# Scores on four 64x64 tiles of TensorE, stack transfers in halves, seven stretches of scores per batch

## The reference

```python
q = (x @ wq.T).reshape(Bx, Tx, H, Dh).transpose(0, 2, 1, 3)   # k, v likewise; H = 16, Dh = 8, Tx = 256
attn = jnp.einsum('bhqd,bhkd->bhqk', q, k) / scale
attn = attn + slopes[None, :, None, None] * dist[None, None, :, :]   # dist = -|key - query|
attn = jax.nn.softmax(attn, axis=-1)
out = jnp.einsum('bhqk,bhkd->bhqd', attn, v)
x = _layernorm(x + out.transpose(0, 2, 1, 3).reshape(Bx, Tx, H * Dh) @ wo.T + bo)
x = _layernorm(x + ffn(x))    # silu gate, two gelu layers, down projection
```

## Time and profile before

| | us |
|---|---|
| median of three runs | 845.25 (842.99 to 847.95) |
| the profiled execution | 847.85 |
| its span in the profile | 846.0 |

### The profile page before, as it was taken

The page is one execution under the profiler, slowest core; times in us unless marked ns, Lnnn a source line. Parts: engine busy times, 40 slices in busy tenths (PEclk is TensorE's granted clock), DMA queues, the critical chain, the costliest instruction groups (busy, mean ns, idle before and its releaser), DMA issues.

```text
span 846.0 us, 22833 instructions
## 1 busy us (share of the span) xinstructions
PE 795.7 (94%) x8322; PEld 582.6 (69%) x8322; DVE 632.1 (75%) x1298; ACT 607.0 (72%) x1099; POOL 311.4 (37%) x488
## 2 busy tenths in 40 slices
PE   4889998999999999998999979999999999999994
PEld 2556666667666666666666558888888888888873
DVE  4768897889888888887888355777777777777774
ACT  3557776767777777776777777777777777777762
POOL 3436776868655555656453310000000000000001
PEclk9999999999999999999999999999999999999997
DMA  6676677776666756676651100111111111111001
GB/s 176 132 159 137 167 155 168 151 172 147 153 139 148 156 146 151 135 159 134 160 128 30 52 21 30 33 37 37 37 37 37 37 33 35 33 36 38 26 26 51
DMA packets 102173, 81.21 MB, mean 96 GB/s; under 512 B 11840, under 2 KB 94912, under 8 KB 102080
## 3 DMA queue, kind: packets, MB, share of 16 engines
q1 hardware_dynamic: 100480, 76.59, 38.8%
q0 software_dynamic: 880, 2.88, 1.8%
q10 hardware_dynamic: 720, 0.46, 0.2%
HBM read 45.82 MB, written 33.55 MB: 94 GB/s over the span
## 4 chain that ended last, share of the span: by engine, by line
PE 91%; DVE 4%; issue 2%; DMA 1%; ACT 1%; SPq 0%; POOL 0%; DVEq 0%; POOLq 0%
PE ps_b L947 16%; PE ps_b L950 16%; PE ps_o L524 15%; PE ps_a L464 11%; PE ps_b L472 5%; PE ps_a L479 4%; PE ps_b L580 4%; PE ps_b L479 3%; DVE neg_sb L759 3%; PE ps_a L950 3%; PE ps_a L947 3%; PE ps_b L541 2%; PE ps_a L563 2%; PE ps_a L549 2%; PE ps_b L535 1%
## 5 line engine op out<-in xcount | busy, mean ns | idle before, releaser
L759 DVE TENSOR_REDUCE neg_sb<-ps_a 128x2 f32<-128x512 f32 x512 | 326.4, 684 | 72.4 <-PE ps_a L479 69.7
L653 ACT ACTIVATE probs<-ps_b 128x512 f32<-128x512 f32 x512 | 270.8, 594 | 90.3 <-PE ps_b L479 89.8
L464 PE MATMUL ps_a<-qk_stack 52*128 52x256 bf16 x1024 | 187.8, 277 | 21.4 <-DMA qk_stack<-qk_scratch 7.5
L472 PE MATMUL ps_b<-qk_stack 54*128 54x256 bf16 x1024 | 182.5, 273 | 0.8 <-ACT probs L653 0.8
L1042 ACT ACTIVATE gelu_f<-ps_b,sc 128x512 f32<-128x512 f32 x128 | 88.2, 689 | 76.8 <-PE ps_b L950 69.3
L479 PE MATMUL ps_a<-corner_sb,eye_sb 64*128 64x128 bf16 x1024 | 141.4, 220 | 0.0
L524 PE MATMUL ps_o<-probs,v_aug 128*32 128x256 f32 x2048 | 138.5, 387 | 1.1 <-issue 1.1
L479 PE MATMUL ps_b<-corner_sb,eye_sb 64*128 64x128 bf16 x1024 | 138.4, 216 | 0.0
L464 PEld LDWEIGHTS ps_a<-qk_stack 52*128 52x128 bf16 x1024 | 68.3, 95 | 90.2 <-issue 51.2
L1152 POOL TENSOR_SCALAR vareps_f<-meanvar_f 128x4 f32<-128x4 f32 x16 | 9.9, 617 | 319.4 <-DVE meanvar_f L1138 319.4
L479 PEld LDWEIGHTS ps_a<-corner_sb,eye_sb 64*128 64x128 bf16 x1024 | 97.7, 97 | 8.6
(11 more groups left out here) (112 smaller groups left out, 1459.8 us busy)
## 6 DMA issues: line engine op xcount, KB each, us to landing
qk_stack<-qk_scratch SPq DMA_DIRECT2D x62, 384.0 KB, 6.3
qk_scratch<-qk_sb SPq DMA_DIRECT2D x64, 192.0 KB, 2.3
qk_scratch<-qk_sb SPq DMA_DIRECT2D x96, 128.0 KB, 2.4
xT_sb<-in_xT SPq DMA_DIRECT2D x32, 128.0 KB, 4.0
qk_stack<-mrow SPq DMA_DIRECT2D x256, 2.0 KB
x_sb<-in_x SPq DMA_DIRECT2D x32, 128.0 KB, 3.7
x_scratch<-x_sb SPq DMA_DIRECT2D x32, 128.0 KB, 3.5
x_in<-x_scratch SPq DMA_DIRECT2D x32, 128.0 KB, 2.1
```

The costliest lines, as they stand in the source:

```text
L464: pe.matmul(ps[:, qb * SEQ:(qb + 1) * SEQ], q_stack[i][rows_of, j, qb * P:(qb + 1) * P], k_stack[i][rows_of, j, :], start=(qb == 0), stop= ...
L472: pe.matmul(ps[:, kb * SEQ:(kb + 1) * SEQ], k_stack[i][rows_of, j, kb * P:(kb + 1) * P], q_stack[i][rows_of, j, :], start=(kb == 0), stop= ...
L653: nc.scalar.activation(probs[:, h % HALF, :], ps_b[b_bank(t, k)][:], ACT.Exp, scale=slope[h]).then_inc(exp_done, 1)
L759: nc.vector.tensor_reduce(negmax[:, h_a // HALF, h_a % GROUPS, h_a % HALF // GROUPS, :], ps_a[a_bank(t, k)][:].rearrange("p (b k) -> p b k ...
```

## The change

Eight edits, all in the attention part:

1. Every score product is cut into two of 64 output partitions (`side` 0 and 1), for `score_max` and `score_exp` both, so a slot has eight matmuls of 256 columns in place of four. `add_corner` keeps its four matmuls of 128 columns, but each has 64 output partitions and a 64-wide unit matrix. All twelve go to 64x64 tiles.
2. `AT` is another table: `v` and `wo` behind slot 1 (and `wo` first), `turn norm` behind 8, `pv 1` behind 10, `qk` and `max 1` behind 13. The scores fall into seven stretches of 2, 3, 2, 2, 2, 3 and 2 slots.
3. `stack` moves a half of the heads in two transfers of 192 KB. The first half is issued where the stack was; the second half at the start of the next step, behind the maxima.
4. `spill(t + 3)` waits for the stacks of batch `t + 1` (the last that used this scratch buffer), no longer for those of `t + 2`.
5. `max_rows` issues two transfers of 4 KB in place of four of 2 KB.
6. ScalarE copies the first maxima behind its slot 3 (was 6), and the second behind slot 14 (was 12); q and k behind 13 (was 12).
7. VectorE adds the residual at slot 1 (was 2) and sums the statistics at 11 (was 5).
8. The last `wo` takes a bank by a rule of its own, since the table moved.

```diff
-AT = {"v": 2, "wo": 2, "pv 3": 4, "max 0": 6, "turn o": 6, "pv 0": 6, "turn norm": 9, "pv 1": 9, "qk": 12, "max 1": 12, "pv 2": 15}
+AT = {"v": 1, "wo": 1, "pv 3": 4, "max 0": 6, "turn o": 6, "pv 0": 6, "turn norm": 8, "pv 1": 10, "qk": 13, "max 1": 13, "pv 2": 15}
...
-            def stack(i, par):
...
+            def stack(b, half):
+
+                src = qk_dram[b % 2].rearrange("n r d (g h j) t -> h g (r d) n (j t)", g=GROUPS, h=2)
                 for g in range(GROUPS):
...
+                    dst = qk_stack[b % STACKS][g * TILE:g * TILE + STACK, :, half * HH:(half + 1) * HH, :]
+                    sp.dma_start(dst.rearrange("p n j t -> p n (j t)"), src[half, g]).then_inc(stacked[b % 2][half], DMA)
...
                 for r in range(MPARTS):
-                    for g in range(GROUPS):
-                        row = g * TILE + MROW + r
-                        dst = qk_stack[i][row:row + 1, 0, hf * HH:(hf + 1) * HH, :]
...
+                    dst = qk_stack[i][MROW + r:P:TILE, 0, hf * HH:(hf + 1) * HH, :]
+                    sp.dma_start(dst.rearrange("g h (b q) -> g (h b) q", b=BLK),
+                                 mrow[hf][:, r, :]).then_inc(m_landed[hf], DMA)
...
+                if live(t + 2, BATCH) and t + 2 > 0:
+                    stack(t + 2, 1)
...
                 if live(t + 3, BATCH):
-                    wait(sp, stacked, (t + 3) * GROUPS * DMA)
+                    for half in range(2):
+                        wait(sp, stacked[1 - par][half], (t + 3) // 2 * GROUPS * DMA)
                     spill(t + 3, 1 - par)
...
-            def score_max(ps, i, h, qb):
+            def score_max(ps, i, h, qb, side):
...
-                rows_of = slice(g * TILE, g * TILE + KA)
-                pe.matmul(ps[:, qb * SEQ:(qb + 1) * SEQ], q_stack[i][rows_of, j, qb * P:(qb + 1) * P],
+                rows_of, at = slice(g * TILE, g * TILE + KA), qb * P + side * TILE
+                pe.matmul(ps[side * TILE:(side + 1) * TILE, qb * SEQ:(qb + 1) * SEQ], q_stack[i][rows_of, j, at:at + TILE],
                           k_stack[i][rows_of, j, :], start=(qb == 0), stop=False, skip_group_check=True)
...
                 for half in range(BLK):
-                    if in_a:
-                        score_max(to_a, i_a, h_a, half)
-                    if in_b:
-                        score_exp(to_b, s, k, half)
+                    for side in range(2):
+                        if in_a:
+                            score_max(to_a, i_a, h_a, half, side)
+                        if in_b:
+                            score_exp(to_b, s, k, half, side)
...
-                    if k == 6 and live(t + 1, BATCH):
+                    if k == 3 and live(t + 1, BATCH):
                         copy_max(t, 0)
...
-                    if k == 12 and live(t + 1, BATCH):
+                    if k == 14 and live(t + 1, BATCH):
                         copy_max(t, 1)
...
-                    if k == 5 and live(t - 2, BATCH):
+                    if k == 11 and live(t - 2, BATCH):
                         sum_stats(t, par)
```

More of the change, by code:

```diff
@@ L121, in a_bank, with spare_bank @@
 def a_bank(t, use):
+    if (t, use) == (BATCH + 1, "wo"):
+        return next(i for i in range(A_BANKS) if i not in (a_bank(BATCH, "turn o"), spare_bank()))
     return (t * len(A_USES) + A_USES.index(use)) % A_BANKS
+def spare_bank():
+    return next(i for i in range(A_BANKS) if i not in (a_bank(BATCH, "wo"), a_bank(BATCH, "turn o")))
 def b_bank(t, use):
@@ L290, in attention @@
         spilled = sem("spilled")
-        stacked, half_stacked = sem("stacked"), sem("half_stacked")
+        stacked = [[sem(f"stacked{i}_{half}") for half in range(2)] for i in range(2)]
         v_done, v_copied = sem("v_done"), sem("v_copied")
@@ L307, in attention @@
         FIRST, LAST = -4, BATCH + 1
-        X_BANK = next(i for i in range(A_BANKS) if all(
-            a_bank(t, use) != i for t, use in ((BATCH, "wo"), (BATCH, "turn o"), (BATCH + 1, "wo"))))
+        X_BANK = spare_bank()
         pieces = []
@@ L405, in step @@
                         sp.wait_ge(rows_laid[t + 3], 2)
+                    stack(t + 3, 0)
                     if t + 3 == 0:
-                        stack_first(0)
-                        stack_first(1)
-                    else:
-                        stack((s + 3) % STACKS, 1 - par)
+                        stack(0, 1)
                 if t == BATCH - 1:
@@ L430, in take_a @@
             def take_a(t, use):
+                if (t, use) == (BATCH + 1, "wo"):
+                    wait(pe, res_done, BATCH - 1)
+                    return ps_a[a_bank(t, use)]
                 before = last_use(t, use, A_USES, A_BANKS, a_batch, FIRST)
@@ L487, in scores @@
                 if in_a:
-                    if h_a == 0 and b_a == 0:
-                        pe.wait_ge(half_stacked, GROUPS * DMA)
-                    elif h_a == (0 if b_a > 0 else HALF):
-                        wait(pe, stacked, (b_a + 1) * GROUPS * DMA)
+                    if h_a % HALF == 0:
+                        wait(pe, stacked[b_a % 2][h_a // HALF], (b_a // 2 + 1) * GROUPS * DMA)
                     to_a = take_a(t, k)
@@ L598, in step @@
                     scores(t, s, k)
+                    if k == AT["wo"] and live(t - 2, BATCH):
+                        project_out(t)
                     if k == AT["v"] and live(t, BATCH):
                         project_v(t)
[L601 to L602 removed]
                     if k == (3 if t < 0 else AT["max 0"]) and live(t + 1, BATCH):
@@ L670, in step @@
                         copy_oT(t)
-                    if k == 12 and live(t + 4, BATCH):
+                    if k == 13 and live(t + 4, BATCH):
                         wait(act, qk_done, t + 5)
@@ L761, in step @@
                                                 AX_X, ALU.max, negate=True).then_inc(max_done, 1)
-                    if k == 2 and live(t - 2, BATCH):
+                    if k == 1 and live(t - 2, BATCH):
                         if t == FLAG_AT:
@@ L820, in split_max @@
                 wait(pool, m_copied, b * 2 + hf + 1)
-                wait(pool, m_landed[hf], b * MPARTS * GROUPS * DMA)
+                wait(pool, m_landed[hf], b * MPARTS * DMA)
                 nc.gpsimd.tensor_copy(mrow[hf][:, 0, :], max_f[hf][:]).then_inc(m_first, 1)
@@ L1199, in shape_constants @@
     corner[:, :, 1, 0], corner[:, :, 1, 1] = above.T, above
-    eye = np.eye(P, dtype=np.float32).reshape(2, TILE, P).transpose(1, 0, 2)
     qscale = np.tile(1.0 / (np.array(slopes()).reshape(HG, GROUPS).T.reshape(-1) * np.sqrt(float(DH))), DH).astype(np.float32)
@@ L1204, in shape_constants @@
         "ident": np.eye(P, dtype=np.float32),
-        "eye": np.concatenate([eye] * GROUPS, 0),
+        "eye": np.tile(np.eye(TILE, dtype=np.float32), (GROUPS, 1)),
         "corner": corner.reshape(P, 2, 2, TILE),
```

32 lines of the change are left out of this document (10 added, 22 removed).

## The result

| | before | after |
|---|---|---|
| median, us | 844.12 (837.12 to 847.95) | 811.3 (810.1 to 813.78) |
| the profiled execution | 847.85 | 810.1 |
| its span | 846.0 | 808.3 |

The account below looks back on a forecast made before the run. TensorE's 13.36 us attention step, plus waits for maxima on SP's equally long loop, was taken as the bound; 847.85 - 23.0 (step) - 12 (waits) = 812.9, less 2.6 for the profiled execution: 810 us, range 797 to 838.

Parts of the forecast that it names:

- The slot: TensorE's scores: corners take one pass instead of two, so a slot falls from 0.335 to 0.285 us, 0.80 us a step.
- Rival (2): Weight loads of 64 columns cost like float32: slot 0.317 us, 829 to 836 us in all; chance 0.12.
- rival (4): Slower: row and column tiles together don't run side by side, loads or matmuls; 940 to about 1000 us; chance 0.10.
- The seventh stretch: TensorE leaves the scores once more in each attention step, charged at 0.08 us a step, between 0.03 and 0.15.
- VectorE's slack: VectorE's attention work, 11.9 us a step, fits the new step of 12.64 us with 0.7 us to spare.
- Rival (3): Slot falls but step doesn't, as VectorE or GpSimd and SP take over: steps 13.1 to 13.3 us, 824 us; chance 0.12.
- The waits: TensorE's waits for maxima at slots 0 and 8: 12 of 17.4 us gained, from below 5 to above 17.
- stand behind half as many bytes: Second-half maxima on the DMA engines: stack landing of 6.5 us ahead of them becomes some 3.3.
- The wait for the last stacks: SP's first-half maxima no longer stand behind this wait, up to 3.1 us.
- The fewer issues: SP issues each set of maxima in two in place of four, 1.35 us less; SP's step 10.2 us, below 12.64.
- the two terms: Attention gains added up: net 23.0 us from slot and seventh stretch over 32 steps, and 12 us of waits.
- The DMA engines' share of 0.66 rises to 0.72: DMA engines' busy share in the attention, with all bytes as before.

Follow-up runs that it names:

- six_stretches: Changed kernel with `turn norm` and `pv 1` behind slot 9, `qk` and `max 1` behind 12, `pv 2` behind 14, ScalarE's copies to match: 814.3 us.
- halves_together: Changed kernel with both halves of a stack issued together where the whole stack was, four transfers of 192 KB: 810.9 us.
- whole_stacks: Changed kernel with a stack read back whole again, two transfers of 384 KB with 4 KB packets in the old place: 837.0 us.
- spill_waits_last: Changed kernel with the old, stricter wait: the spill of batch t + 3 waits also for both halves of the stack of t + 2: 825.2 us.
- maxima_alone: Kernel before with the maxima in two transfers and nothing else: 833.2 us.
- transfers_alone: Kernel before with only edits 3 to 5 (stacks in halves, relaxed spill wait, maxima in two issues): 828.5 us.
- tiles_alone: Kernel before with only edit 1, the twelve 64x64 matmuls a slot; old table, transfers and slots: 853.6 us.

## Why the forecast was right, and where its reasons were not

**The slot** was forecast at 0.285, a gain of 0.80 us a step: it is 0.278 (from 0.334), 16 x 0.056 = 0.90. The load was taken as near 94 ns and is 106; hidden, as argued. Rival (2), a slot of 0.317, and rival (4), tiles or loads one behind the other, are out by the row at 278.71.

**The seventh stretch** was forecast at 0.08 us: 7 x 0.123 - 6 x 0.102 = 0.25. The way out of a stretch had been taken as unchanged, and it grew. Before, a bank wait of some 0.07 us stood in slots 13 to 15, which I had not seen. 0.90 - 0.25 + 0.07 = 0.72, which is the 0.73 found: 22.6 us against 23.0 forecast. Two errors of 0.1 cancelled.

**VectorE's slack**: 338 of 370 us busy, and the step still 12.63. Rival (3) is out. Where it binds is not in the sum but at single banks, as `six_stretches` shows.

**The waits** were forecast at 12 of the 17.4 us, and are 12.9 of 18.0 in the profiled executions; by the medians the whole gain is 5 us smaller than theirs, so that the size is right to within that. Of its three reasons, one is shown not to matter: the maxima of the second half "stand behind half as many bytes". `halves_together` puts the whole stack's bytes ahead of them again and is as fast (810.9); its transfers land in 3.9 us, where those of `whole_stacks` take 6.0. The wait for the last stacks is worth 14 us on the changed kernel, by `spill_waits_last`; on the kernel before, `maxima_alone` keeps it, with whole stacks, and is 5 us behind `transfers_alone`. The fewer issues were put at "1.35 us less" in a row of 10.2 us with room, and are worth 11 us on the kernel before and 37 on the changed one: they are the heart of it.

**The step of the argument that failed** is that the two terms were summed as if each stood alone. The tiles alone lose 10 us. A faster slot brings every deadline forward by 0.7 us a step, and twelve matmuls in place of eight bring more packets of instructions, and in `tiles_alone` both show: 8.6 us of semaphore waits and 15.8 us of stops with none. Neither stood in the prediction as a cost. The sum was right because the change does both; nothing in the prediction said that it had to.

**"The DMA engines' share of 0.66 rises to 0.72"** was false: 0.55. It was worked out from bytes, and a stack's packets of half the bytes took a third of the time.

## What to carry to other kernels

Before a faster engine is credited with its gain, look at what feeds it at fixed places: a queue of issues that is full on the mean but for some 1.5 us has no slack, since one issue of 2 us in place of 0.5 passes straight to the engine that waits. Change the feed and the engine together, and test each alone. Where a stop has no semaphore and lies in the middle of a product, look at the instruction queue's packets and at the size of the data packets beside them. A tiling must hold for all the matmuls of a stretch, since here one change of shape costs 0.1 us and the tiles save 0.056 us a slot.

## What was not expected of the hardware

- Packets of 4096 bytes in the stack transfers took 340 to 352 ns each, those of 2048 bytes 108 to 124: a third of the time for half the bytes. Why is open; 512 bytes took 28 ns and 1024 some 60.
- TensorE stopped 0.3 to 2.6 us at places without any wait, many of them some 245 matmuls (two instruction packets) apart, 1.2 to 1.7 us behind the end of a 16 KB instruction packet, and nearly always where a stack's packets were on the DMA engines beside it. The profile books such a stop as "issue" or to a transfer that has no part in it.
- A weight load of 64 bfloat16 columns on a 64x64 tile takes 105 to 109 ns, one of 128 columns on a 64x128 tile 94.
- Changing between 64x128 and 64x64 tiles costs about 0.1 us each time.
- An issue of SP for maxima into one partition took 0.67 us, for two partitions 0.52; single issues of a spill took up to 1.9 and 2.2 us.
